# Rotary query preparation in two product groups with a stream shuffle, instead of three product groups

## The reference, cut to what matters

```
q = rms_norm(x @ w_qa) @ w_qb                 # per head: 128 plain features, 64 rotary features
q_rope = q_rope * cos + rotate_half(q_rope) * sin
rotate_half(x): out[2i] = -x[2i+1], out[2i+1] = x[2i]
scores = causal(q . k) / sqrt(192); attn = softmax(scores); out = attn @ v
```

## Time and profile before

| what | us |
|---|---|
| median of 3 runs (lowest, highest) | 1176.46 (1174.42, 1178.78) |
| the profiled execution, its own time | 1178.33 |
| its span, first to last instruction | 1176.4 |
| PE busy | 1114.3 |
| DVE busy | 818.9 |
| ACT busy | 791.4 |
| POOL busy | 699.2 |

### The profile page before, as it was taken

One profiled execution on the slowest core, in us unless ns is written; L12 is line 12 of the kernel. 1 busy time (PEld: TensorE's weight loads), 2 busy tenths in 40 slices (PEclk: granted clock), 3 DMA queues, 4 the chain that ended last, 5 costly groups with the idle time before them and its releaser, 6 DMA issues. The chain is left out here.

```text
span 1176.4 us, 27725 instructions
## 1 busy us (share of the span) xinstructions
PE 1114.3 (95%) x11356; PEld 930.9 (79%) x11356; DVE 818.9 (70%) x1825; ACT 791.4 (67%) x1104; POOL 699.2 (59%) x579
## 2 busy tenths in 40 slices
PE   5769999999999999999999999999999788999997
PEld 4747788888888888888888888888887687989886
DVE  3778767676767777676767778677676566675776
ACT  3737777877778787778778787877877543333232
POOL 1436776877777677877676776868777662130000
PEclk9889999999999999999999999999999989999999
DMA  9430100010002000100100020010000050000000
GB/s 241 111 116 17 32 20 9 12 48 20 20 2 65 2 20 26 41 20 2 54 12 20 1 65 15 6 48 20 19 2 2 15 166 1 1 19 1 19 18 18
DMA packets 58126, 39.60 MB, mean 34 GB/s; under 512 B 8113, under 2 KB 57329, under 8 KB 57841
## 3 DMA queue, kind: packets, MB, share of 16 engines
q1 hardware_dynamic: 56608, 33.81, 10.3%
q10 hardware_dynamic: 1392, 4.03, 1.3%
HBM read 33.37 MB, written 4.46 MB: 32 GB/s over the span
## 5 line engine op out<-in xcount | busy, mean ns | idle before, releaser
L912 POOL TENSOR_TENSOR pt_lo<-pt 128x1024 f16<-128x1024 f32 x192 | 370.4, 1940 | 182.1 <-ACT pt L969 181.8
L1031 DVE TENSOR_REDUCE gates<-bank 128x1 f32<-128x512 f32 x384 | 261.6, 689 | 147.8 <-PE bank L1113 144.9
L960 ACT ACTIVATE pair<-shift 128x1024 f32<-128x1024 f32 x256 | 263.5, 1029 | 12.5 <-ACT pt L973 0.7
L969 ACT ACTIVATE pt<-pair 128x1024 f32<-128x1024 f32 x192 | 196.0, 1021 | 110.0 <-PE pair L1141 109.3
L1156 PEld LDWEIGHTS bank<-values,pt 128*128 128x128 bf16 x2176 | 196.8, 98 | 80.4 <-issue 52.5
L1156 PE MATMUL bank<-values,pt 128*128 128x65 f16 x2176 | 235.2, 195 | 6.2 <-DVE lat L1057 5.5
L1158 PE MATMUL bank<-values,pt 128*128 128x64 f16 x2176 | 231.8, 192 | 0.0
L1160 PE MATMUL bank<-values,pt_lo 128*128 128x65 f16 x2176 | 230.8, 194 | 0.0
L918 POOL TENSOR_TENSOR pt_lo<-pt 128x512 f16<-128x512 f32 (+3 forms) x256 | 178.3, 723 | 46.4 <-ACT pt L973 46.3
L1158 PEld LDWEIGHTS bank<-values,pt 128*128 128x128 bf16 x2176 | 202.0, 98 | 0.0
L1160 PEld LDWEIGHTS bank<-values,pt_lo 128*128 128x128 f16 x2176 | 201.3, 97 | 0.0
(11 more groups left out here) (222 smaller groups left out, 2291.4 us busy)
## 6 DMA issues: line engine op xcount, KB each, us to landing
turn_by<-rope_cos_by_feature SPq DMA_DIRECT2D x64, 128.0 KB, 3.0
turn_by<-rope_sin_by_feature SPq DMA_DIRECT2D x64, 128.0 KB, 3.0
xs<-in_L_attn_x SPq DMA_DIRECT2D x4, 512.0 KB, 12.1
lat<-in_L_attn_w_o SPq DMA_DIRECT2D x1, 2048.0 KB, 9.5
xs_again<-in_L_attn_x SPq DMA_DIRECT2D x1, 2048.0 KB, 7.9
out<-xs_again SPq DMA_DIRECT2D x4, 512.0 KB, 2.8
lat<-in_L_attn_w_qb ACTq DMA_DIRECT2D x1, 1152.0 KB, 12.4
wq_parts<-wq_hi SPq DMA_DIRECT2D x1, 1152.0 KB, 7.3
```

Of the source, the lines that this page charges most:

```text
L912: pool.tensor_tensor(out=pt_lo[at][:, :, :].rearrange("p a n -> p (a n)"), in0=full, in1=cut(full), op=ALU.subtract).then_inc(low_ok, 1)
L960: act.activation(s_pair[u % 2][:, :, :], shift_of(item, 1).to_broadcast([P, 2, BW]), ACT.Copy).then_inc(seeded["a"], 1)
L969: act.activation(pt[at][:, :, :], s_pair[u % 2][:, :, :], ACT.Exp).then_inc(exp_done, 1)
L1031: dve.tensor_reduce(out=to, in_=of, axis=AXX, op=ALU.max).then_inc(work_seen["v"], 1)
```

## The change

The weights of the third product group are gone. Part 0 now gives the rotary rows of both heads in one bank, part 1 the plain rows of both. The swap of neighbouring rows is done after the product: DVE multiplies the bank by the sine, with the swap already applied to the sine table (`sin_swapped`, made once by two DMAs) and a sign per row (`sign`), into `by_sin`; it multiplies the bank by the cosine in place; it swaps neighbouring rows of `by_sin` with a stream shuffle; and it adds bank and `by_sin` into `qf`. All five instructions stand in the round of part 0. ACT copies both plain parts in the round of part 1. `wait_seen` of a part 0 is now the wait for the two sums.

```diff
-PT_RING, SHIFTS, Q_SLOTS, MAXIMA = 4, 4, 3, 4
+PT_RING, SHIFTS, Q_SLOTS, MAXIMA = 4, 3, 3, 4
...
-PREP_AT = {r + n: (p, n) for p, r in enumerate(PREP_ROUND) for n in range(4)}
+PREP_AT = {r + n: (p, n) for p, r in enumerate(PREP_ROUND) for n in range(3)}
...
-    return {"max": "v", "shift": "a", "q": "va"}[use[0]] if use[0] != "q" or use[2] < 2 else ""
+    return {"max": {"v": 1}, "shift": {"a": 1}, "q": {"a": 2} if use[-1] else {}}[use[0]]
...
         def wait_seen(eng, n):
             use = WORK_ORDER[n]
-            if use[0] == "q" and use[2] == 2:
+            if use[0] == "q" and use[2] == 0:
                 eng.wait_ge(q_sum, 2 * use[1] + 2)
...
-                def query_turn(p, part):
-                    n = WORK[("q", p, part)]
-                    if part == 0:
-                        if p > 0:
-                            dve.wait_ge(q_lo_ok, 2 * p)
-                        dve.wait_ge(turn_in[p % 2], 64 * (p // 2 + 1))
+                def query_turn(p):
+                    n = WORK[("q", p, 0)]
+                    dve.wait_ge(turn_in[p % 2], 64 * (p // 2 + 1))
+                    if p == 0:
+                        dve.wait_ge(before["sign_ok"], 4)
+                    else:
+                        dve.wait_ge(q_sum, 2 * p)
                     dve.wait_ge(work_done, n + 1)
...
+                    dve.scalar_tensor_tensor(out=by_sin[:, :], in0=work_of(n)[:, :], scalar=sign[:, :], in1=turn_by[:, p % 2, 1, :],
+                                             op0=ALU.mult, op1=ALU.mult).then_inc(q_turned, 1)
+                    dve.tensor_tensor(out=work_of(n)[:, :], in0=work_of(n)[:, :], in1=turn_by[:, p % 2, 0, :],
+                                      op=ALU.mult).then_inc(q_turned, 1)
+
+                def query_swap(p):
+                    dve.wait_ge(q_turned, 2 * p + 1)
+                    dve.stream_shuffle(by_sin[:, :], by_sin[:, :], [i ^ 1 for i in range(32)]).then_inc(q_swapped, 1)
 
                 def query_sum(p):
...
+                    if p > 0:
+                        dve.wait_ge(q_lo_ok, 2 * p)
+                    dve.wait_ge(q_swapped, p + 1)
+                    dve.wait_ge(q_turned, 2 * p + 2)
+                    by_cos = work_of(WORK[("q", p, 0)])
                     for hd in range(2):
-                        dve.tensor_tensor(out=qf[ROT[hd], hd, :], in0=by_sin[ROT[hd], :], in1=qf[ROT[hd], hd, :],
+                        dve.tensor_tensor(out=qf[ROT[hd], hd, :], in0=by_cos[ROT[hd], :], in1=by_sin[ROT[hd], :],
                                           op=ALU.add).then_inc(q_sum, 1)
...
                     p, part = PREP_AT.get(r, (0, 3))
-                    if part < 3:
+                    if part < 2:
                         query_products(p, part)
```

More of the change, by code:

```diff
@@ L330, in sync @@
             sp.dma_start(wov, k["w_o"].rearrange("(h p) n -> p h n", p=P)).then_inc(ld_o, 16)
+            to, of = (w.rearrange("(i e) s -> e i s", e=2) for w in (k["sin_swapped"], k["sin_t"]))
+            for e in range(2):
+                sp.dma_start(to[e], of[1 - e]).then_inc(sines_out, 16)
         def store_query_weights(sp):
@@ L442, in rotary_weights @@
                 act.wait_ge(ld_qb, 16)
-                act.wait_ge(qscale_ok, 2)
-                for at, e, of, minus in those:
-                    act.activation(pair_cols(wq_hi, at, e), of, ACT.Copy, scale=(qscale, qminus)[minus][:, 0:1]).then_inc(wqh_ok, 1)
+                act.wait_ge(qscale_ok, 1)
+                for at, e, of in those:
+                    act.activation(pair_cols(wq_hi, at, e), of, ACT.Copy, scale=qscale[:, 0:1]).then_inc(wqh_ok, 1)
             def twins(b):
@@ L514, in vector @@
             dve.memset(norms[0:KVL, 2:3], 1.0).then_inc(ones_ok, 1)
+            for n, with_sign in enumerate((1.0, -1.0)):
+                dve.memset(picked[:, 0, :].rearrange("p (i e) -> p i e", e=2)[:, :, n], with_sign).then_inc(sign_ok, 1)
+            dve.wait_ge(sign_ok, 2)
+            dve.wait_ge(consts, 8)
+            dve.tensor_tensor(out=picked[:, 1, :], in0=picked[:, 0, :], in1=ident[:, :], op=ALU.mult).then_inc(sign_ok, 1)
+            dve.wait_ge(sign_ok, 3)
+            dve.tensor_reduce(out=sign[:, :], in_=picked[:, 1, :], axis=AXX, op=ALU.add).then_inc(sign_ok, 1)
             dve.wait_ge(silu_c, 1)
@@ L551, in rotary_low @@
             def rotary_low(first, last):
-                for n, (at, e, of, minus) in list(enumerate(moves))[first:last]:
+                for n, (at, e, of) in list(enumerate(moves))[first:last]:
                     dve.wait_ge(wqh_ok, n + 1)
                     hi = pair_cols(wq_hi, at, e).bitcast(F32)
-                    dve.scalar_tensor_tensor(out=pair_cols(wq_lo, at, e), in0=of, scalar=(qscale, qminus)[minus][:, 0:1], in1=hi,
+                    dve.scalar_tensor_tensor(out=pair_cols(wq_lo, at, e), in0=of, scalar=qscale[:, 0:1], in1=hi,
                                              op0=ALU.mult, op1=ALU.subtract).then_inc(wql_ok, 1)
@@ L648, in vector @@
             scaled(3)
-            rotary_low(4, 8)
             columns(1)
@@ L859, in shift_of @@
             at = item % SHIFTS
-            return shift[at // 2][:, at % 2:at % 2 + half, :]
+            return shift[:, at:at + half, :]
         def work_of(n):
@@ L926, in _, with query_plain @@
                         query_low(p)
+                    if part == 2 and p == 0:
+                        pool.wait_ge(before["wq_out"], 32)
+                        pool.memset(ones_r[:, :].bitcast(F32), 1.0).then_inc(consts_ok, 1)
             @block.scalar
             def _(act):
-                def query_plain(p, part):
-                    n = WORK[("q", p, part)]
-                    if part == 0 and p > 0:
+                def query_plain(p):
+                    n = WORK[("q", p, 1)]
+                    if p > 0:
                         act.wait_ge(q_lo_ok, 2 * p)
                     act.wait_ge(work_done, n + 1)
-                    act.activation(qf[PLAIN[part], part, :], work_of(n)[PLAIN[part], :], ACT.Copy).then_inc(work_seen["a"], 1)
+                    for hd in range(2):
+                        act.activation(qf[PLAIN[hd], hd, :], work_of(n)[PLAIN[hd], :], ACT.Copy).then_inc(work_seen["a"], 1)
                 def query_high(p):
+                    wait_seen(act, WORK[("q", p, 1)])
                     if p >= Q_SLOTS:
@@ L1035, in item_shift @@
                     wait_seen(dve, WORK[("max", FIRST_CHUNK[item + 1] - 1)])
+                    if item == 0:
+                        dve.wait_ge(before["wq_out"], 32)
                     dve.tensor_reduce(out=nmx[:, item % 2, :], in_=mx[:, item % MAXIMA, :, 0:g + 1], axis=AXX, op=ALU.max,
```

106 lines of the change are left out of this document (44 added, 62 removed).

## The result

| | before | after |
|---|---|---|
| median (lowest, highest), us | 1176.04 (1174.42, 1178.78) | 1240.61 (1239.12, 1241.6) |
| profiled execution, own time | 1178.33 | 1240.2 |
| its span | 1176.4 | 1238.4 |

Both medians are of four runs each, on the same chip. The ratio is 1.0546 (95% interval 1.053 to 1.0563): the change makes the kernel 5.5% slower. I had predicted slower, but 1212 with a range of 1201 to 1230.

What follows compares the result with a forecast made beforehand. PE was taken as the bound, full from pair 4 to 31. 1178.3 - 19.6 (part 2 gone) + 55.4 (wait for the bank) + 0 (first four pairs) = 1214.1, or 1212 as median; range 1201 to 1230.

Steps and rivals of the forecast that it cites:

- the clock: Rival: PE's clock falls in the new idle times, 1.7 us each, 1260 if all; chance 0.05 for most, 0.10 a third.
- clock under 1.0 in the middle slices: Sign that the prediction is wrong: PE below full clock in the middle of the profile.
- The wait: PE before part 1, held until DVE's five query instructions (3.54 us) free the bank: 1.98 us per pair, 55.4 for 28.
- rival of a cheap shuffle: DVE's shuffle takes between nothing and 0.5 us: 20 us off at most, 1192 to 1206; chance 0.10.
- that of a shuffle held by POOL: POOL holds the shuffle or a chain instruction, up to 0.7 us more each, or 1.4: 1232; chance 0.08.
- The gain: Part 2's three products leave PE, 0.70 us per pair in pairs 4 to 31: 19.6 us gained.
- No second wait behind the first: After the wait before part 1, PE meets no other; work queued behind DVE's chain has more than a round to spare.
- The first four pairs: Pairs before PE is full: taken as 0 together, with ends of -3 and +3 us.
- `prepare`: Scaling instructions that leave and the sign's four there count as nothing; under 2 us if their cover were gone.

Runs made afterwards that it cites:

- e3_fill: The changed kernel with 14 products of 252 columns that nobody reads put on PE ahead of part 1 from pair 4 on; 1219.11 us, ratio 1.0343.
- e8_split: The changed kernel with the cosine product in SBUF, and the shuffle and adds one round later behind that round's maxima; 1170.28 us, ratio 0.9942.
- e6_less: The kernel before, with part 2 made by one product instead of three, the two correcting products left out; 1167.93 us, ratio 0.9924.
- e1_swap: The changed kernel with the plain rows made first (part 0) and the rotary rows second (part 1); 1190.04 us, ratio 1.0113.
- e4_noshuf: The changed kernel with the stream shuffle left out, so the rotary rows are wrong; 1198.74 us, ratio 1.0175.
- e5_shuf3: The changed kernel with the shuffle made three times, each waiting for the one before, output the same; 1332.02 us, ratio 1.1305.

## Why the prediction was wrong

**The step that failed** is the clock. I wrote "I take some of them at most, since the first product behind and the scores around keep PE dense", gave most falls 0.05 and a third 0.10, and closed the range at 1230. There were 16 falls in 28 waits. Their price I had nearly right (1.7 from the earlier trace rows, measured 1.53); their number I had not. 1214.1, my sum for the profiled execution, and 24.5 make 1238.6, against 1240.2. `e3_fill` shows it by taking the falls alone away. And the reason that I gave does not hold: PE was dense behind the waits, and the falls began up to 1.5 us into that dense work. Of the signs of being wrong, "clock under 1.0 in the middle slices" came, though only windows show it. In the earlier trace rows I had one idle time without a fall and one with, of nearly the size of the new ones. Two such rows are no ground for "some at most"; they were one in two, which gives 1214 + 14 x 1.7 = 1238. That this is so near is luck: the idle time of 1.80 us at 919.17 stands at the same place in all ten kernels, 1.80 long each time, and a fall followed in three of them (before, `e3_fill`, `e8_split`). In the kernel after it did not:

```profile
982.80 0.20 PE L1167 MATMUL bank<-values,pt 128*128 128x65 f16 x1 [1.80 <-DVE lat L1066]
...
983.10:986.50 3.40, 3.40 (x57) 2.87 (x52) 1.77 (x7) 1.06 (x2) 1.06 (x1) 1.00 0.02 5
```

**The wait** was right: 28 x 1.98 = 55.4 predicted, so 53.5 for the 27 waits of the stretch, and 53.6 measured; part 1 at +4.09 where the sum 0.54 + 3.54 + 0.05 gives 4.13. The single terms, with the group rows of the kernel after:

```profile
L1010 DVE SCALAR_TENSOR_TENSOR by_sin<-bank,sign,turn_by 128x512 f32<-128x512 f32 x32 | 24.0, 749 | 3.7 <-PE bank L1112 2.1
L1017 DVE STREAM_SHUFFLE by_sin<-by_sin 128x512 f32<-128x512 f32 x32 | 23.2, 726 | 0.0
L1012 DVE TENSOR_TENSOR bank<-bank,turn_by 128x512 f32<-128x512 f32 x32 | 22.0, 688 | 0.0
```

The shuffle takes 0.726 where I took 0.70 from the copy of its shape, and the following add starts 0.82 behind its start. The Trainium skill's price (VectorE: DVE Perf Modes, "The perf-mode tier table"), from which I had estimated 0.60, does not agree with this row. A part of the time that does not shrink with the length would explain it; no run here has a second length to show that. The rival of a cheap shuffle fell with it, and that of a shuffle held by POOL too: the 32 instances of L1017 take 0.71 to 0.75.

**The gain** was right in its price (27 x 0.70 goes into an account that closes within 1.6), and `e6_less` shows such a gain alone, less a quarter that comes back (3.4 of 12.6).

**"No second wait behind the first"** was off by 3.4 us: `evacuate`, which I had listed as queued behind the chain with more than a round to spare, was asked for too early at six places, by 0.64 us each where it was 0.07. In `e1_swap` the same queue costs some 18. **The first four pairs** and `prepare` were put at 0 and gave -0.8. All of it is small beside the clock.

**Still open:** which of the idle times bring a fall. By the idle record of the kernel after, 2 of 6 of 1.60 were followed by one, 7 of 8 of 1.71 to 1.73, 5 of 5 of 1.80, but only 2 of 6 of 1.92 to 1.94, and none of the three of 1.1 to 1.2. Length alone doesn't order those between 1.6 and 1.94, nor does the place in the order of work: pairs 6, 10, 14, 18, 22 and 26 stand in equal rounds with equal idle times, and only 10 and 26 have a fall. Nor is 1.80 a length that always brings one: in `e1_swap` 2 of 6 idle times of 1.80 to 1.81 in the stretch did, and one of 1.92. Not tried either: `e8_split` with adds that have an operand in PSUM, which would keep them free of POOL.

## What to carry to other kernels

Where an engine is full, ask of each wait that a change puts on it not only how long it is but what the engine's clock does behind it: if the trace shows one idle time of that size with a fall and one without, it doesn't say how many will have one (16 of 25 here, 3 of 7 in `e1_swap`). Put some of the falls into the sum and all of them into the range, and don't count on dense work behind the wait to keep them away. Before giving up a change that adds such a wait, look for what holds the shared buffer (here, one output moved out of PSUM took 61.5 us off a stretch that had become 64.2 longer), and then read what the same instructions delay in the engine's own order, because that is where the rest of the gain stays.

## What the runs showed of the hardware that I had not expected

- Idle times of PE of only 1.6 to 1.94 us, in a stream that is full before and behind, brought the clock to its lower level for 3.4 us in 16 of 25 cases, at 1.53 us each. In 15 of the 16 the fall began when PE had been at work again for 0.2 to 1.5 us. The same idle time of 1.80 us at the same place was followed by a fall in three of the ten kernels. With 1.33 and less none of 28 did (`e4_noshuf`), with 2.6 to 3.8 every one did (`e5_shuf3`).
- Work that nobody reads made the kernel faster: 14 products of 252 columns in each wait, 1.79 us, took 23.9 us from the stretch and brought the median from 1240.6 to 1219.1.
- A DVE instruction with two operands in SBUF can last until an instruction of POOL ends: two adds took 2.99 us instead of 1.41, `spread` 2.38 where its median is 0.69, and POOL's own `pt_lo` 2.38 instead of 1.9 when the add had begun first. The Trainium skill says so (SBUF — State Buffer, "SBUF: two separate sides"): the pair of ports that the two share is held by one for a whole instruction. The trace agrees, with both DVE records ending 0.55 us behind POOL's.
